# Sorting stage of a graph kernel: the rank one-hots of 10 of 36 columns are made on ScalarE, those of the other 26 on VectorE

## What is computed

```python
h = jnp.maximum(_layernorm(x, axis=-1), 0.0)
x = x + segment_sum(h[src], dst, num_segments=6250)
h = jnp.maximum(_layernorm(x, axis=-1), 0.0)
out = h; y = h
for l in range(3):
    f1 = relu(y[src] @ nb_W[l] + nb_b[l]);  f2 = relu(y[dst] @ self_W[l] + self_b[l])
    a = relu(concatenate([f1, f2], axis=1) @ att1_W[l] + att1_b[l]) @ att2_W[l] + att2_b[l]
    mask = clip(sigmoid(a) * (1.05 + 0.45) - 0.45, 0, 1)
    d = clip((segment_sum(mask, src) + 1e-6) ** -0.5, 0, 10)
    y = segment_sum(mask * d[src] * d[dst] * y[dst], src);  out = out + y
return x + out
```

## Time and profile before

| | |
|---|---|
| median of 3 runs | 4017.64 us (4015.11 to 4019.21) |
| profiled execution, its own time | 4011.47 us |
| its span | 4009.5 us, 257,956 instructions |
| mean granted TensorE clock | 0.969 of full speed |
| TensorE matmul / VectorE / ScalarE / GpSimd busy | 3713.7 / 3249.0 / 1983.1 / 2387.6 us |
| the sort's 49 rows in the trace | about 34 us to 457 us, a tenth of the span |

### The profile page before, as it was taken

One profiled execution on the slowest core, in us unless ns is written; L12 is line 12 of the kernel. 1 busy time (PEld: TensorE's weight loads), 2 busy tenths in 40 slices (PEclk: granted clock), 3 DMA queues, 4 the chain that ended last, 5 costly groups with the idle time before them and its releaser, 6 DMA issues. The chain is left out here.

```text
span 4009.5 us, 257956 instructions
## 1 busy us (share of the span) xinstructions
PE 3713.7 (93%) x99855; PEld 3566.9 (89%) x99856; DVE 3249.0 (81%) x5352; ACT 1983.1 (49%) x5442; POOL 2387.6 (60%) x4694
## 2 busy tenths in 40 slices
PE   6999678888779999999998999999998999999998
PEld 5888578888769999899988999999997999989998
DVE  7999868888768888788877888878886888878887
ACT  2222368888721111488871111178884111138887
POOL 3777523333235666677774666667775566657776
PEclk8999799999989999999999999999999999999999
DMA  1111289999837777677746777757773777767775
GB/s 39 16 16 16 55 288 342 337 332 338 286 120 248 248 246 240 188 190 190 190 124 205 248 246 240 254 157 190 190 190 118 239 244 241 246 196 190 190 190 157
DMA packets 586318, 800.05 MB, mean 200 GB/s; under 512 B 126839, under 2 KB 528203, under 8 KB 586219
## 3 DMA queue, kind: packets, MB, share of 16 engines
q1 hardware_dynamic: 550154, 719.89, 57.5%
q0 software_dynamic: 36064, 78.85, 6.6%
HBM read 672.34 MB, written 126.04 MB: 199 GB/s over the span
## 5 line engine op out<-in xcount | busy, mean ns | idle before, releaser
L1388 PE MATMUL pre_ps<-rows_a,hot_ab 128*128 128x64 bf16 x21609 | 1297.6, 194 | 48.2 <-ACT rows_a L1481 23.2
L1388 PE MATMUL pre_ps<-table,hot_ab 128*128 128x64 bf16 x21609 | 1296.3, 194 | 0.8 <-issue 0.8
L1388 PEld LDWEIGHTS pre_ps<-rows_a,hot_ab 128*128 128x128 fp8e4 x21609 | 1129.7, 98 | 77.4 <-issue 54.2
L1622 POOL TENSOR_TENSOR message<-message 128x448 f32<-128x448 f32 x1029 | 947.2, 932 | 320.5 <-DVE message L1690 320.0
L1388 PEld LDWEIGHTS pre_ps<-table,hot_ab 128*128 128x128 fp8e4 x21609 | 1131.3, 98 | 0.6 <-issue 0.6
L1672 DVE SCALAR_TENSOR_TENSOR message<-pre_ps,all_w 128x448 f32<-128x448 f32 x1029 | 642.3, 624 | 277.0 <-PE pre_ps L1388 198.6
L1432 PE MATMUL pre_ps<-table,hot_ab 128*128 128x64 bf16 x21609 | 803.9, 194 | 18.0 <-DVE message L1690 9.5
L1432 PEld LDWEIGHTS pre_ps<-table,hot_ab 128*128 128x128 fp8e4 x21609 | 762.5, 98 | 20.6 <-issue 20.3
L1529 ACT ACTIVATE message<-pre_ps 128x448 bf16<-128x448 f32 x1029 | 673.2, 674 | 167.2 <-DVE pre_ps L1684 139.0
L1684 DVE TENSOR_TENSOR pre_ps<-pre_ps,mask 128x448 f32<-128x448 f32 x735 | 464.7, 632 | 206.8 <-PE pre_ps L1432 184.2
L1655 DVE TENSOR_REDUCE logit<-message 128x7 f32<-128x448 f32 x1029 | 626.2, 609 | 0.0
(11 more groups left out here) (193 smaller groups left out, 4847.2 us busy)
## 6 DMA issues: line engine op xcount, KB each, us to landing
hot_ab<-hot_scratch SPq DMA_DIRECT2D x2058, 224.0 KB, 4.0
hot_scratch<-hot SPq DMA_DIRECT2D x343, 336.0 KB, 5.9
both<-hot_scratch SPq DMA_DIRECT2D x147, 784.0 KB, 5.1
places<-slots_scratch POOLq DMA_DIRECT2D x196, 224.0 KB, 6.5
places<-slots_scratch POOLq DMA_DIRECT2D x98, 336.0 KB, 7.4
slots_scratch<-bins SPq DMA_DIRECT2D x392, 16.0 KB, 1.4
out<-res SPq DMA_DIRECT2D x3, 416.0 KB
raw<-in_src SPq DMA_DIRECT2D x1, 768.0 KB
```

Of the source, the lines that this page charges most:

```text
L1388: last = nc.tensor.matmul(pre_ps[g][:, j, :], hot[:, b, g, end, j * P:(j + 1) * P].bitcast(FP8), table, start=end + part == 0, stop=end == ...
L1622: pool.tensor_tensor(message[:, g, :, 2, :], message[:, g, :, 1, :], top[:, g, :, 1, :, 1], ALU.subtract).then_inc(s["third_ready"], 1)
```

## The change

Columns 0 to 25 (BY_DVE = 26) are compared on VectorE as before, in an instruction with 26 x 128 = 3328 elements a partition where there were 36 x 128 = 4608; `rank_four` shrinks to 26 columns. For the last ten columns (BY_ACT = 10) ScalarE makes ten instructions `square`, each of 128 elements: (rank - number)^2, with the rank as a bias read from a column of `rank_few`. One more instruction of 10 x 128 = 1280 elements, Relu of 1 - square, gives `spread_more`, which is 1 where the two are equal and 0 elsewhere. `spread_more` has two buffers. The squares stand between `rank_four` and `sooner_w` in ScalarE's order, the Relu between `sooner_w` and `block_four`. The scatter waits for `more_spread` as well, and its last ten matmuls read `spread_more`.

```diff
-        rank_four = sb("rank_four", [P, 2, WIN, FOUR], BF16)
+        rank_four = sb("rank_four", [P, 2, BY_DVE, FOUR], BF16)
-        spread = sb("spread", [P, WIN, P], BF16)
+        spread = sb("spread", [P, BY_DVE, P], BF16)
+        square = sb("square", [P, BY_ACT, P], BF16)
+        spread_more = sb("spread_more", [P, 2, BY_ACT, P], BF16)
...
                 def scatter(c, b):
                     pe.wait_ge(s["values_ready"], c + 3)
                     pe.wait_ge(s["spread"], c + 3)
+                    pe.wait_ge(s["more_spread"], c + 1)
                     pe.wait_ge(s["bins_ready"], c + 1)
                     hold_waits(pe, s)
                     for w in range(WIN):
-                        last = nc.tensor.matmul(bins_ps[b][:, :], value[:, b, w, :], spread[:, w, :],
+                        slots = spread[:, w, :] if w < BY_DVE else spread_more[:, b, w - BY_DVE, :]
+                        last = nc.tensor.matmul(bins_ps[b][:, :], value[:, b, w, :], slots,
                                                 start=w == 0, stop=w == WIN - 1)
...
+                def square_offsets(c, b):
+                    act.wait_ge(s["ranks_wide"], c + 3)
+                    if not isinstance(c, int) or c > 0:
+                        act.wait_ge(s["more_spread"], c)
+                    for w in range(BY_ACT):
+                        last = nc.scalar.activation(square[:, w, :], k.ranks[:, :], ACT.Square, scale=-1.0,
+                                                    bias=rank_few[:, b, BY_DVE + w:BY_DVE + w + 1])
+                    last.then_inc(s["offsets_squared"], 1)
+
+                def spread_rest(c, b):
+                    act.wait_ge(s["offsets_squared"], c + 1)
+                    act.wait_ge(s["scattered"], c + 1)
+                    nc.scalar.activation(spread_more[:, b, :, :], square[:, :, :], ACT.Relu, scale=-1.0, bias=k.ones[:, 0:1])\
+                        .then_inc(s["more_spread"], 1)
+
                 def row(c, b, nth, first):
...
                     nc.scalar.activation(rank_few[:, b, :], rank_ps[b][:, :], ACT.Copy)
-                    nc.scalar.activation(rank_four[:, b, :, :], rank_ps[b][:, :].unsqueeze(2).to_broadcast([P, WIN, FOUR]),
+                    nc.scalar.activation(rank_four[:, b, :, :], rank_ps[b][:, 0:BY_DVE].unsqueeze(2).to_broadcast([P, BY_DVE, FOUR]),
                                          ACT.Copy).then_inc(s["ranks_wide"], 1)
+                    square_offsets(c, b)
                     take_prefix(c + 1, 1 - b)
+                    spread_rest(c, b)
                     widen_blocks(c + 2, b)
```

More of the change, by code:

```diff
@@ L369, in sort_edges @@
         TURN = WIN - GROUPS
+        BY_ACT = 10
+        BY_DVE = WIN - BY_ACT
         local = sb("local", [P, 2, WIN + TURN], BF16)
@@ L393, in fours, with along @@
             return t.rearrange("p w (m f) -> p w m f", f=FOUR)
-        def along(four, m):
-            return four.unsqueeze(2).to_broadcast([P, WIN, m, FOUR])
+        def along(four, m, n=WIN):
+            return four.unsqueeze(2).to_broadcast([P, n, m, FOUR])
         def later_columns(b):
@@ L400, in later_columns @@
             return bass.AP(row.tensor, row.offset, [row.ap[0], [GROUPS, COLS - 1], [1, WIN]])
-        with phase(nc, "passed keyed placed blocks_wide places_wide hot_ready twins_ready values_ready prefixed prefix_ready "
+        with phase(nc, "offsets_squared more_spread passed keyed placed blocks_wide places_wide hot_ready twins_ready values_ready prefixed prefix_ready "
                        "picked folded ranked ranks_wide spread scattered bins_ready noted stored0 stored1 "
@@ L607, in spread_out @@
                     dve.wait_ge(s["scattered"], c + 2)
-                    nc.vector.tensor_tensor(fours(spread[:, :, :]), fours(k.ranks[:, :].unsqueeze(1).to_broadcast([P, WIN, P])),
-                                            along(rank_four[:, b, :, :], P // FOUR), ALU.is_equal).then_inc(s["spread"], 1)
+                    nc.vector.tensor_tensor(fours(spread[:, :, :]), fours(k.ranks[:, :].unsqueeze(1).to_broadcast([P, BY_DVE, P])),
+                                            along(rank_four[:, b, :, :], P // FOUR, BY_DVE), ALU.is_equal).then_inc(s["spread"], 1)
                 def row(c, b, nth, first):
```

## The result

The changed kernel takes 4032.93 us, the median of 6 runs (4024.18 to 4033.95), against 4018.03 (4014.57 to 4024.07): ratio 1.0035, 95% interval 1.0024 to 1.0045, so 14 to 15 us or 0.35% slower. Timed again on another occasion (run after_again) the ratio was 1.0034 (1.0024 to 1.0044). The forecast was 4027.5 us, 10 us slower.

A forecast was written before the change was run, and what follows sets the result against it. The prediction took VectorE to limit warm sort rows and TensorE at a lowered clock the cold ones. ScalarE's lateness, 10.5 us taken, less 0.65 gave about 10 us slower: 4017.6 to 4027.5 us, own range 4021 to 4032, whole range 4012 to 4036.

The forecast's parts named there:

- VectorE's saving: In the sort, VectorE compares 1280 fewer elements, 0.65 us a row; with nothing else changed, 5 us in all at most.
- The squares' pace: ScalarE's ten squares in a row start 0.29 us apart, 2.9 us for ten; the other bound was 2.53 us.
- Rival 1: Squares follow each other closer, 0.253 us apart, so warm rows stay as long as now: 4016 us; chance 0.15.
- Ranks to `sooner_w`: ScalarE's chain from ranks to `sooner_w` takes 3.28 us in even rows, 3.38 in odd; 0.44 and 0.59 late in warm rows.
- Relu and `block_four`: After `sooner_w` on ScalarE, the Relu takes 1.36 us and delays `block_four`, done by 2.0 us: hidden, 0.3 us to spare.
- Rival 4: ScalarE's late `block_four` binds as well: 0.2 us a row, 4037 us; chance 0.05.
- Cold rows: Sort rows with TensorE's granted clock lowered to 0.81, 9.1 us each, stay: 20 to 23 of 46.
- Rival 3: Longer TensorE idle lets the clock fall in warm rows' places too: 26 us over the forecast, 4053 us; chance 0.05.
- The bound of idle: TensorE's clock falls behind idles of 0.69 us or more ahead of the rank matmuls, not behind 0.61 or 0.62.
- rival 2: Squares under 0.235 us apart, ScalarE never late, TensorE's idle shorter, 8 cold rows: 24 us less, 3993 us; chance 0.09.
- The sum: Over the sort's 46 rows, 8.4 to 11.7 us more; 10.5 taken less 0.65, about 10 us slower.
- the ring: Sort's row loop from TensorE's line 474 to ScalarE's `sooner_w` and on: 7.55 us even, 7.44 odd without VectorE's limit.

The follow-up runs named there:

- scalar_only: The changed kernel with VectorE comparing all 36 columns again, ScalarE's squares and Relu kept, the scatter reading only VectorE's result: ratio 1.0030 to the kernel before.
- vector_only: The changed kernel without squares, Relu and the wait for them; the last ten columns read a buffer of zeros: ratio 0.9986 to the kernel before.
- moved: The changed kernel with squares and Relu moved behind `place_four` in ScalarE's order, no longer between ranks and `sooner_w`: ratio 0.9984 to the kernel before.
- by8: The changed kernel with eight columns on ScalarE instead of ten, in the same place: ratio 0.9985 to the kernel before.
- busy_before: The kernel before with eight unread matmuls of 128 columns added at the start of each row on TensorE: ratio 0.9924 to the kernel before.
- busy_after: The changed kernel with eight unread matmuls of 128 columns added at the start of each row on TensorE: ratio 1.0034 to the kernel before.
- busy_moved3: The changed kernel with squares and Relu behind `place_four` and three unread matmuls at each row's start on TensorE: ratio 0.9949 to the kernel before.

## Why the prediction was right, and where it was not

- **VectorE's saving**: forecast 0.65 us a row and worthless while `sooner_w` is late. `spread` fell by 0.67 (2.549 to 1.878), and scalar_only shows the worth in this kernel: none. The prediction's remark that the saving with nothing else changed is worth 5 us at most was wrong: vector_only brought 9.6, with 17 cold rows in place of 20. About half is warm rows of 7.5 us, as forecast, the other half the cold rows that the prediction had said would stay.
- **The squares' pace**: taken 0.29 us, from two instructions out of SBUF with 64 columns and a slope, against 0.253 from the PSUM rows. Measured 0.295. Rival 1 rested on the PSUM rows, and is out. The Trainium skill's figure ("ScalarE: Activation LUTs", section "What ACT_TABLE_LOAD costs") had led to an estimate of 294 ns; this trace agrees, with 295.
- **Ranks to `sooner_w`**: forecast 3.28 and 3.38 us, measured 3.32 and 3.40. Warm rows 7.99 and 8.03, measured 8.00 and 8.03. ScalarE's wait for its own `rank_four` was 0.04 as taken (320.65 to 320.69).
- **Relu and `block_four`**: hidden, as forecast. `block_four` ends 1.95 us after `sooner_w` starts (325.58), `hot_w` starts 2.35 after. Rival 4 is out.
- **Cold rows**: forecast between 20 and 23, so 390.9 to 394.2 us for the 46 rows, 10.5 us more taken. Measured 24 and 23, 394.7 and 392.9: 12.1 and 10.4 more against the first trace. Against the mean of the two traces of before they are 11.3 and 9.5 more. Alternation is strict but for rows 10 and 11, both cold (without exception in after_again), the upper end of the forecast, and the table above shows why: behind an idle of 1.17 us or more every one of 87 rows was cold, so each warm row of about 8 us brought a cold one after it. The idles had been forecast rightly, 1.16 and 1.20 against 1.18 and 1.20. Rival 3, still more cold rows, came only as far as one.
- **The bound of idle**: here the prediction's reading was wrong. "Ahead of the rows in which it had idled only 0.61 or 0.62 the clock did not fall" was true of one trace, and I read it as a clear bound. Those rows all followed cold rows, and such rows were seldom cold whatever their idle, so they told little. Moved, vector_only, by8, the second trace of before and row 2 of the changed kernel have cold rows behind 0.62 to 0.64. It didn't touch the forecast, whose idle was 1.2, but rival 2 was mis-sized by it: its 24 us rested on 8 cold rows, and by8 and moved, the kernels in which its condition holds, had 18 and 17 and gained 8 to 10 us in the sort.
- **The sum**: 10 us against 8.6 and 10.8 at the end of the sort. The median moved 14.9 us to 4032.93, inside the whole range of 4012 to 4036 but 1 us above the forecast's own, 4021 to 4032. The mechanism accounts for some 10 of these; about 5 lie behind the sort, where the prediction had put nothing ("The other stages have no part in it"). They are the open point above, and that the time still fell within the range is in part luck.

## What to carry to other kernels

Half idle is not free: ask between which two events the idle time lies. ScalarE stood idle for nearly 80% of the sort and could take eight squares between the ranks and the counts, or ten behind them; two squares too many between an engine's two handovers of the ring cost 19 to 20 us (by8 against the changed kernel, in the 46 rows), where the busiest engine's saving alone had given 9.6. When a stage's rows come in two lengths, look at the granted clock before the code, and before you read a bound from what stood ahead of the slow ones, see whether the fast ones with the same idle could have been slow at all: here nearly all of them followed a cold row.

## What had not been expected of the hardware

Matmuls that nobody reads, 0.6 us of them in a gap of 0.6 to 0.95 us, made the whole kernel 0.76% faster (busy_before), since 20 of 46 rows last 7.67 us on average in place of 9.13. The effect comes within a few tenths of a us of idle: in busy_after 0.73 us were left, and the matmuls had no effect at all; in busy_moved3 0.56, and half of the cold rows were gone; with 0.51 or less all of them. And GpSimd's busy time fell, though nothing was changed there: 270.3 us in the 46 rows before, 209.0 in the changed kernel. scalar_only differs from the changed kernel in VectorE's compare alone, has rows of the same length, and shows 258.2. So 49 of the 61 us come with the size of the compare beside which GpSimd works; by which mechanism no run shows, and none of it was on the path.
